# Value products of sixteen attention heads: padded 128-column weights per head against four 32-column strips per group of four heads

## The chip, the cores and the metric

The kernel runs on one NeuronCore of one Trainium2 chip. The metric is the device time of one execution in microseconds (us), from the start of the program to its end on that core; the number given for a kernel is the median of its runs.

## What is computed

Eight sequences of 512 tokens by 512 features pass through four layers. The part that matters here is the attention of the second layer; around it lie a small adapter with a layer norm (before), a feed-forward layer, a second feed-forward layer and a finite-difference stencil (after). Cut to the attention:

```python
x = _ln(src) * (1.0 + scale) + shift
q = (x @ Wq + bq).reshape(B, S, N_HEAD, HEAD_DIM).transpose(0, 2, 1, 3)      # B 8, S 512, 16 heads of 32
k = ...; v = (x @ Wv + bv).reshape(B, S, N_HEAD, HEAD_DIM).transpose(0, 2, 1, 3)
scores = jnp.einsum('bhqd,bhkd->bhqk', q / math.sqrt(HEAD_DIM), k)
scores = scores + attention_bias
scores = jnp.where(src_mask, -jnp.inf, scores.astype(jnp.float32))
probs = jax.nn.softmax(scores, axis=-1).astype(v.dtype)
ctx = jnp.einsum('bhqk,bhkd->bhqd', probs, v)
ctx = ctx.transpose(0, 2, 1, 3).reshape(B, S, D)
x = x + (ctx @ Wo + bo)
```

## The kernel before

The program has two passes. `attention_pass` loops over the eight sequences (adapter, attention, output projection) and writes its rows to memory; `ffn_pass` then does the rest. The change lies in `attention_pass` alone.

Every fp32 operand of a large product is split into two fp16 halves, "hi" and "lo", and a product is three matmuls: hi by hi, hi by lo, lo by hi (the helper `three`).

One iteration of the loop, on TensorE (`pe`): projections q, k, v; transposes of the next sequence's input and its "down" product; then a loop over slots `n` of `SLOTS_ALL` = 75; then the transposes `x1T` of the next sequence and the output projection (`wo`). A slot stands for one head `h` = n // 4 and one block `j` = n % 4 of 128 query rows (there are 64 such blocks). The engines run the same slots in their own program order, tied by semaphores:

- TensorE, slot n: the scores S(n) (two matmuls into one of three PSUM banks 0 to 2: the mask, then q by k), in some slots a product of the next sequence's adapter (`PE_L0`: "up" at 8, 10, 12, 14), the transposes T(n-5) of four probability tiles into a bank of the ring 3 to 5 that the adapter products use too, and the value products PV.
- VectorE (`dve`), slot n: adds the bias to S(n) and takes the row maximum (`negs`, `nmax`), adapter work of some slots (`DVE_L0`: "y" at 9, 11, 13, 15; layer-norm statistics at 19, 21, 23, 25 and 45, 47, 49, 51), then `pT_lo` of T(n-5).
- ScalarE (`act`), slot n: copies T(n-5) from PSUM into `pT_hi`, then the exponential `prob` of S(n), then adapter work (`ACT_L0`: scales at 31, 33, 35, 37 and 56, 58, 60, 62).

The value products give ctx with the features of four heads (a group g) on the 128 partitions of one PSUM bank (6 or 7). A head has only 32 features, so the weights `v_pad` hold, for each head, 128 columns of which 32 are the head's values and 96 are zeros that GpSimd sets once; all matmuls of the group add into the whole bank. They are spread evenly: slot n does key block j of head h for (h, j) = n - 7, three matmuls, and waits for `pT_split` of that block. `pT` holds two heads. When the group's last product is in (`pv_done`), VectorE scales ctx (line 944, slot `ctx_slot(g)` = 16(g+1)+9), ScalarE makes its hi half (line 755, end of that slot) and VectorE its lo half (line 950, start of the next slot). ScalarE waits once per head for `pv_done` before it overwrites `pT_hi`.

`claim` is TensorE's wait for the reader of a bank's last content, `arrived` a reader's wait for the bank to be full.

Of the kernel before, what the change touches and what calls it, by code (L numbers as in the profile page):

```python
# [48 lines left out]
PS = 4096.0  # L49
# [39 lines left out]
LAG_PV = 7  # L89
SLOTS_ALL = HT + 11  # L90


def rinv_slot(g):
    return 4 * T * (g + 1) + 2

# [5 lines left out]
def ctx_slot(g):  # L101
    return 4 * T * (g + 1) + LAG_PV + 2

# [10 lines left out]
def attention_slots():  # L114
# [3 lines left out]
    for n in range(SLOTS_ALL):  # L118
# [9 lines left out]
        if 0 <= n - LAG_PV < HT and (n - LAG_PV) % (4 * T) == 0:  # L128
            g = (n - LAG_PV) // (4 * T)
            order.append((("ctx", g), 6 + g % 2))  # L130
        for g in range(G):
            if n == turn_slot(g):
                order.append((("R", g), 3 + ring % 3))
                ring += 1
# [3 lines left out]
def attention_pass(nc, a, ada_rows, x2_dram):  # L138
# [11 lines left out]
    with ExitStack() as ctx:  # L150
# [38 lines left out]
        v_pad = [sb(f"v_{h}", [P, T, H, P], F16) for h in ("hi", "lo")]  # L189
# [13 lines left out]
        pT = [sb(f"pT_{h}", [P, 2, T, S], F16) for h in ("hi", "lo")]  # L203
# [35 lines left out]
        v_zeroed = sem("v_zeroed")  # L239
# [7 lines left out]
        hi_done = sem("hi_done")  # L247
# [33 lines left out]
        prob_ready = sem("prob_ready")  # L281
        pT_split = sem("pT_split")
# [24 lines left out]
        def read_by(key):  # L307

            name, k = key[0], key[-1]
            return {"xT": (xT_split, C, k), "down": (hid_ready, 2, 0), "expert": (hid_ready, 2, 1),  # L310
                    "up": (y_ready, T, k), "x1T": (x1T_split, C, k), "q": (f32_ready, 12, 0),
                    "k": (f32_ready, 12, 4), "v": (f32_ready, 12, 8), "S": (scored, H * T, k),
                    "T": (pT_split, H * T, k), "R": (rinv_T_ready, G, k), "ctx": (ctx_ready, G, k),
                    "wo": (x2_ready, T, k)}[name]

        def claim(pe, it, key):
# [3 lines left out]
            if last[0] in ("q", "k", "v"):  # L320
                k += last[1]
# [14 lines left out]

        def f32_split(n):

            return (qk_split, 2 * C, n + 1) if n < 8 else (v_split, T, n - 7)

# [111 lines left out]
        def _(pool):  # L452
# [6 lines left out]
            for part in v_pad:  # L459
                pool.memset(part[:, :, :, :].rearrange("p t h m -> p (t h m)").bitcast(F32), 0.0).then_inc(v_zeroed, 1)  # L460
# [61 lines left out]
        def _(pe):  # L522
# [52 lines left out]
            pe.wait_ge(v_zeroed, 2)  # L575
            with pe.Fori(0, B) as it:
# [24 lines left out]
                for n in range(SLOTS_ALL):  # L601
# [29 lines left out]
                    for g in range(G):  # L631
                        if n == turn_slot(g):
# [18 lines left out]
        def _(act):  # L651
# [53 lines left out]
            with act.Fori(0, B) as it:  # L705
                def copy_hi(key, dst, scale):
                    bank = arrived(act, it, key)
                    act.activation(dst, bank[:, :], ACT.Copy, scale=scale).then_inc(hi_done, 1)  # L708

                def to_f32(n, key, func, scale, bias_ap):  # L710
                    bank = arrived(act, it, key)
                    split, per, k = f32_split(n - 2 if n >= 2 else 10 + n)
# [1035 lines left out]
```

## Time and profile before

| what | value |
|---|---|
| median of 3 runs | 3039.82 us (3038.07 to 3041.19) |
| the profiled execution: span from first to last instruction | 3036.2 us |
| TensorE matmul busy | 2699.6 us (89%) |
| VectorE busy | 2182.4 us (72%) |
| ScalarE busy | 1320.3 us (43%) |
| GpSimd busy | 919.8 us (30%) |
| mean granted TensorE clock | 0.966 |

The span is 3.6 us below the median of the runs. The profile gives no device time of its own for the profiled execution beside the span; the 3.6 us are taken as what lies around the span. The attention pass fills the first 1,400 us or so. Matmuls are pipelined: a busy time of TensorE counts each matmul with its latency, so the distance from one start to the next tells what a matmul costs in a stream.

### The profile page before, as it was taken

What the parts mean: (1) busy time and instruction counts of PE and PEld (TensorE: products, weight loads), DVE (VectorE), ACT (ScalarE), POOL (GpSimd) and SP (SyncE); (2) the same over time, 40 slices, a digit from 0 to 9 for tenths busy, and PEclk for the clock granted to TensorE, in tenths of its full rate; (3) what the DMA queues carried; (4) which work ended last, traced back from release to release, by engine and by line L of the source; (5) the groups of instructions that cost most, each with busy time, mean ns of one, the idle gap of its engine ahead of it and who ended that gap; (6) DMA issues with size and microseconds to landing.
All of it is one profiled execution on the core that took longest, in us unless ns stands there. A gap on an engine that the chain in (4) does not pass through costs nothing.

```text
span 3036.2 us, 45734 instructions
## 1 busy us (share of the span) xinstructions
PE 2699.6 (89%) x13435; PEld 1352.2 (45%) x13435; DVE 2182.4 (72%) x4261; ACT 1320.3 (43%) x2485; POOL 919.8 (30%) x898
## 2 busy tenths in 40 slices
PE   2799999999999999994889899998999999999991
PEld 1354555555554545452434344443444434444340
DVE  5686868687877868686866767667676675676758
ACT  2584748576675848584322232222322222222220
POOL 3322131212131312213332513325143350433516
PEclk6899999999999999997999999999999999999995
DMA  3444444353535354443421322222222222222212
GB/s 122 145 153 129 153 133 146 126 153 117 159 131 151 140 144 146 131 153 120 156 91 63 121 86 78 95 75 103 86 91 83 85 96 83 91 89 81 92 59 83
DMA packets 182891, 344.54 MB, mean 113 GB/s; under 512 B 20354, under 2 KB 50690, under 8 KB 182674
## 3 DMA queue, kind: packets, MB, share of 16 engines
q1 hardware_dynamic: 172882, 324.31, 32.9%
q10 hardware_dynamic: 9792, 17.83, 1.6%
q8 instruction: 77, 1.26, 0.2%
q14 instruction: 140, 1.15, 0.1%
HBM read 298.85 MB, written 17.86 MB: 104 GB/s over the span
## 4 chain that ended last, share of the span: by engine, by line
PE 24%; issue 13%; DVE 9%; POOL 7%; ACT 1%; DVEq 0%; DMA 0%; POOLq 0%; SPq 0%; ACTq 0%
PE ffn_bank L1335 7%; PE ffn_bank L1337 7%; PE ffn_bank L1336 7%; POOL prod L1256 3%; DVE g2T_hi L1627 2%; DVE wl_lo L1633 1%; POOL f L1246 1%; POOL x L1274 1%; DVE tmp L1537 1%; POOL prod L1267 1%; PE ffn_bank L1328 1%; DVE g2T_lo L1628 1%; PE ffn_bank L1394 1%; PE ffn_bank L1344 0%; DVE tmp L1577 0%
## 5 line engine op out<-in xcount | busy, mean ns | idle before, releaser
L742 ACT ACTIVATE prob<-negs,nmax 128x512 f32<-128x512 f32 x512 | 368.4, 720 | 113.1 <-DVE nmax L962 112.1
L901 DVE SCALAR_TENSOR_TENSOR pT_lo<-bank,pT_hi 128x512 f16<-128x512 f32 x512 | 350.4, 684 | 93.2 <-ACT pT_hi L708 92.1
L962 DVE CUSTOM_DVE_ANT_0 negs<-bank,bias 128x512 f32<-128x512 f32 x512 | 347.6, 682 | 16.4 <-PE bank L606 12.3
L1627 DVE CAST g2T_hi<-g 128x512 f16<-128x512 f32 x256 | 173.1, 676 | 253.2 <-ACT g L1456 249.9
L616 PE MATMUL bank<-ident,prob 128*128 128x128 f32 x2048 | 312.3, 274 | 37.3 <-ACT prob L742 20.9
L616 PEld LDWEIGHTS bank<-ident,prob 128*128 128x128 f32 x2048 | 250.9, 141 | 160.0 <-ACT prob L742 44.4
L708 ACT ACTIVATE pT_hi<-bank 128x512 f16<-128x512 f32 x512 | 298.3, 583 | 54.3 <-PE bank L616 53.3
L1456 ACT ACTIVATE g<-ffn_bank,bi 128x512 f32<-128x512 f32 x128 | 88.0, 687 | 384.4 <-PE ffn_bank L1337 379.4
L1628 DVE TENSOR_TENSOR g2T_lo<-g,g2T_hi 128x512 f16<-128x512 f32 x256 | 239.7, 936 | 8.8
L1335 PE MATMUL ffn_bank<-w_hi,g2T_hi 128*128 128x512 f16 x512 | 197.1, 385 | 48.2 <-DVE g2T_lo L1628 48.0
L1335 PE MATMUL ffn_bank<-x3T_hi,w_hi 128*128 128x512 f16 x512 | 198.5, 388 | 26.5 <-DVE tmp L1577 25.0
L528 PE MATMUL bank<-pT_hi,v_hi 128*128 128x512 f16 x512 | 195.0, 381 | 18.6 <-DVE pT_lo L901 16.7
L1256 POOL TENSOR_TENSOR prod<-grid,f 128x512 f32<-128x512 f32 x108 | 166.5, 1567 | 125.5 <-DMA grid<-in_grids 119.4
L1337 PE MATMUL ffn_bank<-x3T_hi,w_lo 128*128 128x512 f16 x512 | 199.0, 389 | 0.0
L1336 PE MATMUL ffn_bank<-x3T_lo,w_hi 128*128 128x512 f16 x512 | 198.3, 387 | 0.0
L605 PE MATMUL bank<-mask_add,ident_bf 128*128 128x512 bf16 x512 | 194.6, 380 | 2.4 <-DVE nmax L962 2.4
L1336 PE MATMUL ffn_bank<-w_lo,g2T_hi 128*128 128x512 f16 x512 | 196.1, 383 | 0.0
L1337 PE MATMUL ffn_bank<-w_hi,g2T_lo 128*128 128x512 f16 x512 | 195.7, 382 | 0.0
L606 PE MATMUL bank<-k_st,q_st 96*128 96x512 f16 x512 | 195.6, 382 | 0.0
L1335 PE MATMUL ffn_bank<-x3T_hi,wl_hi 128*128 128x512 f16 x512 | 194.2, 379 | 0.5 <-DVE tmp L1577 0.2
L529 PE MATMUL bank<-pT_lo,v_hi 128*128 128x512 f16 x512 | 194.5, 380 | 0.0
L530 PE MATMUL bank<-pT_hi,v_lo 128*128 128x512 f16 x512 | 194.5, 380 | 0.0
(265 smaller groups left out, 5675.5 us busy)
## 6 DMA issues: line engine op xcount, KB each, us to landing
bias<-in_bias SPq DMA_DIRECT2D x256, 512.0 KB, 3.3
raw<-in_W_l SPq DMA_DIRECT2D x128, 512.0 KB, 3.2
grid<-in_grids SPq DMA_DIRECT2D x172, 256.0 KB, 3.0
xin<-in_x SPq DMA_DIRECT2D x9, 1024.0 KB, 5.2
x2n<-x_rows SPq DMA_DIRECT2D x9, 1024.0 KB, 7.0
out<-outt ACTq DMA_DIRECT2D x36, 256.0 KB, 2.0
q_st<-pT_hi SPq DMA_DIRECT2D x64, 128.0 KB, 4.8
k_st<-pT_hi SPq DMA_DIRECT2D x64, 128.0 KB, 2.8
```

The source lines that it names most:

```text
L606: pe.matmul(bank[:, :], q_st[0:96, h, j * P:(j + 1) * P], k_st[0:96, h, :], start=False, stop=True).then_inc(full_of(("S", h, j)), 1)
L616: mm = pe.transpose(bank[:, t * P:(t + 1) * P], prob[:, h % 2, t, j * P:(j + 1) * P], ident[:, :])
L708: act.activation(dst, bank[:, :], ACT.Copy, scale=scale).then_inc(hi_done, 1)
L742: act.activation(prob[:, h % 2, j, :], negs[:, j % NT, :], ACT.Exp, scale=-1.0, bias=nmax[:, h % 2, j:j + 1], accum_out=rsum[:, j, h:h + 1 ...
L901: ins = dve.scalar_tensor_tensor(out=lo, in0=bank[:, :], scalar=scale, in1=hi, op0=ALU.mult, op1=ALU.subtract)
L962: dve.tensor_tensor_reduce(negs[:, j % NT, :], bank[:, :], bias[:, half % NB, j % 2, :], -1.0, 3.0e38, ALU.add, ALU.min, nmax[:, h % 2, j: ...
L1256: pool.tensor_tensor(prod[:, i, :], grid[:, i, :], f[:, t, :], ALU.mult).then_inc(alpha_prod, 1)
L1335: pe.matmul(out, w[0], x[0], start=first, stop=False)
L1336: pe.matmul(out, w[0], x[1], start=False, stop=False)
L1337: return pe.matmul(out, w[1], x[0], start=False, stop=last)
L1627: link(dve.tensor_copy(gT[0][:, n % 4, :], g32[:, n % 2, :]))
L1628: dve.tensor_tensor(gT[1][:, n % 4, :], g32[:, n % 2, :], gT[0][:, n % 4, :], ALU.subtract)\
```

## The change

The value products of one group are taken together at the group's end. For key block kb of group g (slot `pv_slot(g, kb)` = 16g + 20 + kb) TensorE now issues twelve matmuls: for each of the three hi/lo pairs, one matmul for each of the four heads, with weights of 32 columns (`v_sp`, unpadded) and an output of 32 partitions (`bank[32 i : 32 i + 32]`). Every matmul still streams 512 columns over 128 rows, and there are still 192 of them in an iteration. `pT` holds five heads. `pv_done` counts groups instead of heads, and ScalarE waits for it ahead of every copy. `ctx_slot(g)` becomes 16g + 24, one slot earlier than before. GpSimd's two zero fills are gone, and VectorE writes v's halves to contiguous tiles.

```diff
-LAG_PV = 7
+LAG_PV = 3
+RING_H = 5
+def pv_slot(g, kb):
+    return T * (4 * g + 3) + kb + LAG_T + LAG_PV
+def groups_before(h):
+    return (h - RING_H) // 4 + 1 if h >= RING_H else 0
 def ctx_slot(g):
-    return 4 * T * (g + 1) + LAG_PV + 2
+    return pv_slot(g, T - 1) + 1
...
-        v_pad = [sb(f"v_{h}", [P, T, H, P], F16) for h in ("hi", "lo")]
+        v_sp = [sb(f"v_{h}", [P, T, D], F16) for h in ("hi", "lo")]
...
-        pT = [sb(f"pT_{h}", [P, 2, T, S], F16) for h in ("hi", "lo")]
+        pT = [sb(f"pT_{h}", [P, RING_H, T, S], F16) for h in ("hi", "lo")]
...
-            for part in v_pad:
-                pool.memset(part[:, :, :, :].rearrange("p t h m -> p (t h m)").bitcast(F32), 0.0).then_inc(v_zeroed, 1)
...
-                    if 0 <= n - LAG_PV < HT:
-                        h, j = (n - LAG_PV) // T, (n - LAG_PV) % T
-                        key = ("ctx", h // 4)
-                        if h % 4 == 0 and j == 0:
-                            claim(pe, it, key)
-                            pe.wait_ge(v_split, 1 + it * T + T)
-                        bank = psum[banks.place[key][0]]
-                        pe.wait_ge(pT_split, 1 + it * HT + T * h + j + 1)
-                        mm = three(bank[:, :], [v[:, j, h, :] for v in v_pad], [p[:, h % 2, j, :] for p in pT],
-                                   h % 4 == 0 and j == 0, h % 4 == 3 and j == T - 1)
-                        if j == T - 1:
-                            mm.then_inc(pv_done, 1)
                     for g in range(G):
+                        for kb in range(T):
+                            if n != pv_slot(g, kb):
+                                continue
+                            key = ("ctx", g)
+                            if kb == 0:
+                                claim(pe, it, key)
+                                pe.wait_ge(v_split, 1 + it * T + T)
+                            bank = psum[banks.place[key][0]]
+                            pe.wait_ge(pT_split, 1 + it * HT + T * (4 * g + 3) + kb + 1)
+                            for w, x in ((0, 0), (0, 1), (1, 0)):
+                                for i in range(4):
+                                    h = 4 * g + i
+                                    mm = pe.matmul(bank[HD * i:HD * i + HD, :], v_sp[w][:, kb, h * HD:(h + 1) * HD],
+                                                   pT[x][:, h % RING_H, kb, :], start=kb == 0 and w + x == 0,
+                                                   stop=kb == T - 1 and w == 1)
+                            if kb == T - 1:
+                                mm.then_inc(pv_done, 1)
...
-                        if j == 0:
-                            act.wait_ge(pv_done, 1 + it * H + max(0, h - 1))
-                        copy_hi(("T", h, j), pT[0][:, h % 2, j, :], PS)
+                        bank = arrived(act, it, ("T", h, j))
+                        act.wait_ge(pv_done, 1 + it * G + groups_before(h))
+                        act.activation(pT[0][:, h % RING_H, j, :], bank[:, :], ACT.Copy, scale=PS)\
+                            .then_inc(pT_hi_ready, 1)
```

TensorE's order around slots 19 to 21 (the transposes `ident,rinv_x` stand in slot 20). Before, each slot has its three value products:

```order
L605 MATMUL bank<-mask_add,ident_bf 128x512
L606 MATMUL bank<-k_st,q_st 128x512
L616 MATMUL bank<-ident,prob 128x128 x4
L528 MATMUL bank<-pT_hi,v_hi 128x512
L529 MATMUL bank<-pT_lo,v_hi 128x512
L530 MATMUL bank<-pT_hi,v_lo 128x512
L637 MATMUL bank<-ident,rinv_x 128x128 x4
```

The same place after the change, from the scores of slot 19:

```order
L603 MATMUL bank<-mask_add,ident_bf 128x512
L604 MATMUL bank<-k_st,q_st 128x512
L614 MATMUL bank<-ident,prob 128x128 x4
L331 REGISTER_ALU
L603 MATMUL bank<-mask_add,ident_bf 128x512
L604 MATMUL bank<-k_st,q_st 128x512
L614 MATMUL bank<-ident,prob 128x128 x4
L630 MATMUL bank<-pT_hi,v_hi 32x512 x4
L630 MATMUL bank<-pT_lo,v_hi 32x512 x4
L630 MATMUL bank<-pT_hi,v_lo 32x512 x4
L640 MATMUL bank<-ident,rinv_x 128x128 x4
```

Slot 19 now has scores and transposes alone; slot 20 has twelve value products in place of three.

VectorE's order where ctx of group 0 is taken (`L962`, after the change `L945`, is the bias addition of a slot; `L901`, after it `L954`, is pT_lo). Before, slots 25 and 26:

```order
L944 SCALAR_TENSOR_TENSOR ctx<-bank,rinv_T 128x512
L331 REGISTER_ALU
L960 REGISTER_ALU
L962 ISA negs,nmax<-bank,bias 128x512
L962 ISA nmax 128x1
L849 BN_STATS stats<-xin 128x6
L772 REGISTER_ALU
L851 BN_AGGR mv<-stats 128x2
L901 SCALAR_TENSOR_TENSOR pT_lo<-bank,pT_hi 128x512
L949 REGISTER_ALU
L950 SCALAR_TENSOR_TENSOR xT_lo<-ctx,bv,xT_hi 128x512
```

After, slots 24 and 25:

```order
L927 SCALAR_TENSOR_TENSOR ctx<-bank,rinv_T 128x512
L337 REGISTER_ALU
L941 ISA
L943 REGISTER_ALU
L945 ISA negs,nmax<-bank,bias 128x512
L945 ISA nmax 128x1
L954 SCALAR_TENSOR_TENSOR pT_lo<-bank,pT_hi 128x512
L933 SCALAR_TENSOR_TENSOR xT_lo<-ctx,bv,xT_hi 128x512
```

The statistics that stood between ctx and its lo half in slot 25 now stand behind the lo half.

## Rows read from the trace of the kernel before

**Rows 1.** The page, part 5: the engines' idle time before three groups of the slots.

```profile
L901 DVE SCALAR_TENSOR_TENSOR pT_lo<-bank,pT_hi 128x512 f16<-128x512 f32 x512 | 350.4, 684 | 93.2 <-ACT pT_hi L708 92.1
L962 DVE CUSTOM_DVE_ANT_0 negs<-bank,bias 128x512 f32<-128x512 f32 x512 | 347.6, 682 | 16.4 <-PE bank L606 12.3
L708 ACT ACTIVATE pT_hi<-bank 128x512 f16<-128x512 f32 x512 | 298.3, 583 | 54.3 <-PE bank L616 53.3
```

The columns of a window: stretch, its length, busy us (instructions) of PE, PE's weight loads, VectorE, ScalarE, GpSimd, granted clock, DMA share, GB/s.

**Rows 2.** Window of the 75 slots of the fifth iteration.

```profile
622.53:738.00 115.47, 106.38 (x608) 63.07 (x607) 98.14 (x230) 93.42 (x210) 27.07 (x48) 1.00 0.44 146
```

**Rows 3.** Timeline of slots 9 to 12 (start us, us, engine, line).

```profile
635.66 0.69 DVE L845 SCALAR_TENSOR_TENSOR xin<-bank,xin 128x512 f32<-128x512 f32 x1
...
636.40 0.39 PE L528 MATMUL bank<-wup_hi,ctx 128*128 128x512 f16 x1 [0.24 <-DVE xin L845]
...
637.06 0.60 PE L616 MATMUL bank<-ident,prob 128*128 128x128 f32 x4
637.50 0.38 PE L528 MATMUL bank<-pT_hi,v_hi 128*128 128x512 f16 x1
637.70 0.60 ACT L708 ACTIVATE pT_hi<-bank 128x512 f16<-128x512 f32 x1 [1.11 <-PE bank L616]
...
638.15 0.38 PE L605 MATMUL bank<-mask_add,ident_bf 128*128 128x512 bf16 x1
...
638.33 0.69 DVE L901 SCALAR_TENSOR_TENSOR pT_lo<-bank,pT_hi 128x512 f16<-128x512 f32 x1 [0.78 <-ACT pT_hi L708]
...
638.58 0.60 PE L616 MATMUL bank<-ident,prob 128*128 128x128 f32 x4
639.02 0.38 PE L528 MATMUL bank<-pT_hi,v_hi 128*128 128x512 f16 x1
...
639.64 0.69 DVE L845 SCALAR_TENSOR_TENSOR xin<-bank,xin 128x512 f32<-128x512 f32 x1
```

**Rows 4.** Timeline of ScalarE in slot 16.

```profile
649.04 0.60 ACT L708 ACTIVATE pT_hi<-bank 128x512 f16<-128x512 f32 x1 [0.50 <-PE bank L616]
```

**Rows 5.** Timeline of VectorE, slots 19 to 26.

```profile
655.26 0.66 DVE L901 SCALAR_TENSOR_TENSOR pT_lo<-bank,pT_hi 128x512 f16<-128x512 f32 x1
...
658.58 0.66 DVE L901 SCALAR_TENSOR_TENSOR pT_lo<-bank,pT_hi 128x512 f16<-128x512 f32 x1
...
663.69 0.68 DVE L944 SCALAR_TENSOR_TENSOR ctx<-bank,rinv_T 128x512 f32<-128x512 f32 x1
...
665.83 0.66 DVE L901 SCALAR_TENSOR_TENSOR pT_lo<-bank,pT_hi 128x512 f16<-128x512 f32 x1
666.58 0.75 DVE L950 SCALAR_TENSOR_TENSOR xT_lo<-ctx,bv,xT_hi 128x512 f16<-128x512 f32 x1
```

**Rows 6.** Line 950 over the whole program: idle of VectorE before it (us, times).

```profile
  ACT xT_hi L755: 21.4, 24
```

**Rows 7.** Timeline of TensorE around the 8-row matmul of the second pass.

```profile
1522.29 0.38 PE L1328 MATMUL ffn_bank<-msp_lo,dmat 128*128 128x512 f16 x1
1522.60 0.39 PE L1328 MATMUL ffn_bank<-halo,halo_w 8*128 8x512 f16 x1
1522.92 0.39 PE L1335 MATMUL ffn_bank<-x3T_hi,w_hi 128*128 128x512 f16 x1
```

**Rows 8.** Timeline of the end of the slots, VectorE then TensorE.

```profile
736.48 0.69 DVE L901 SCALAR_TENSOR_TENSOR pT_lo<-bank,pT_hi 128x512 f16<-128x512 f32 x1 [0.39 <-ACT pT_hi L708]
...
738.03 1.91 PE L534 MATMUL bank<-ident,xin 128*128 128x128 f32 x16
```

**Rows 9.** Windows, a sparse stretch and its successor, then another sparse stretch.

```profile
229.50:232.90 3.40, 1.56 (x9) 0.47 (x7) 2.54 (x7) 2.79 (x7) 1.20 (x1) 1.00 0.00 0
233.00:236.40 3.40, 3.40 (x12) 2.04 (x13) 2.35 (x7) 3.00 (x7) 2.55 (x2) 0.51 0.02 5
393.40:396.80 3.40, 1.98 (x11) 0.81 (x9) 2.54 (x7) 2.32 (x5) 0.73 (x1) 1.00 0.00 0
```

**Rows 10.** Timeline of GpSimd, its first operation after the zero fills.

```profile
24.48 5.82 POOL L490 TENSOR_TENSOR xin<-xin,up_b 128x512 f32<-128x512 f32 x4 [15.75 <-DMA bo<-in_bo]
```

More of the change, by code:

```diff
@@ L48 @@
 NEG = -1.0e30
-PS = 4096.0
 RSQRT_SEED = 1597463007.0
@@ L127, in attention_slots @@
             ring += 1
-        if 0 <= n - LAG_PV < HT and (n - LAG_PV) % (4 * T) == 0:
-            g = (n - LAG_PV) // (4 * T)
-            order.append((("ctx", g), 6 + g % 2))
         for g in range(G):
+            if n == pv_slot(g, 0):
+                order.append((("ctx", g), 6 + g % 2))
             if n == turn_slot(g):
@@ L281, in attention_pass @@
         prob_ready = sem("prob_ready")
+        pT_hi_ready = sem("pT_hi_ready")
         pT_split = sem("pT_split")
@@ L307, in read_by @@
         def read_by(key):
-            name, k = key[0], key[-1]
+            name, k = key[0], key[-1] if len(key) > 1 else 0
             return {"xT": (xT_split, C, k), "down": (hid_ready, 2, 0), "expert": (hid_ready, 2, 1),
[L311 to L314, printed above, removed]
+                    "up": (y_ready, T, k), "x1T": (x1T_split, C, k), "q": (f32_ready, 12, k),
+                    "k": (f32_ready, 12, 4 + k), "v": (f32_ready, 12, 8 + k), "S": (scored, H * T, k),
+                    "T": (pT_split, H * T, k), "R": (rinv_T_ready, G, k),
+                    "ctx": (ctx_ready, G, k), "wo": (x2_ready, T, k)}[name]
         def claim(pe, it, key):
@@ L808, in weight_lo @@
                                          op0=ALU.mult, op1=ALU.subtract).then_inc(weights_split, 1)
-            def diagonal(v, t):
-                part = v[:, t, :, :]
-                return bass.AP(tensor=part.tensor, offset=part.offset,
-                               ap=[list(part.ap[0]), [4 * P, G], [P + HD, 4], [1, HD]])
             def l0_part(link, it, part):
@@ L893, in _ @@
                 link = chained(it * LINKS_A + before)
-                def lo_of(key, k, hi, lo, signal, scale=None):
-                    bank = psum[banks.place[key][0]]
-                    dve.wait_ge(hi_done, it * (H * T) + k + 1)
-                    if scale is None:
-                        ins = dve.tensor_tensor(lo, bank[:, :], hi, ALU.subtract)
-                    else:
-                        ins = dve.scalar_tensor_tensor(out=lo, in0=bank[:, :], scalar=scale, in1=hi,
-                                                       op0=ALU.mult, op1=ALU.subtract)
-                    ins.then_inc(signal, 1)
                 def split_f32(k, hi, lo, signal):
@@ L924, in _ @@
                     dve.wait_ge(f32_ready, it * 12 + 2 * C + t + 1)
-                    src = f32t[:, t % 2, :].rearrange("p (g i d) -> p g i d", i=4, d=HD)
-                    hi, lo = (diagonal(v, t) for v in v_pad)
-                    link(dve.tensor_copy(hi, src))
-                    dve.tensor_tensor(lo, src, hi, ALU.subtract).then_inc(v_split, 1)
+                    link(dve.tensor_copy(v_sp[0][:, t, :], f32t[:, t % 2, :]))
+                    dve.tensor_tensor(v_sp[1][:, t, :], f32t[:, t % 2, :], v_sp[0][:, t, :], ALU.subtract)\
+                        .then_inc(v_split, 1)
                 dve.wait_ge(v_split, 1 + it * T + T)
@@ L940, in _ @@
                             bank = psum[banks.place["ctx", g][0]]
-                            dve.wait_ge(pv_done, 1 + it * H + 4 * g + 4)
+                            dve.wait_ge(pv_done, 1 + it * G + g + 1)
                             dve.wait_ge(rinv_T_ready, it * G + g + 1)
@@ L968, in _ @@
                         h, j = (n - LAG_T) // T, (n - LAG_T) % T
-                        lo_of(("T", h, j), n - LAG_T, pT[0][:, h % 2, j, :], pT[1][:, h % 2, j, :], pT_split, PS)
+                        bank = psum[banks.place["T", h, j][0]]
+                        dve.wait_ge(pT_hi_ready, it * HT + n - LAG_T + 1)
+                        dve.scalar_tensor_tensor(out=pT[1][:, h % RING_H, j, :], in0=bank[:, :], scalar=PS,
+                                                 in1=pT[0][:, h % RING_H, j, :], op0=ALU.mult, op1=ALU.subtract)\
+                            .then_inc(pT_split, 1)
                 for c in range(C):
```

30 lines of the change are left out of this document (11 added, 19 removed).

## Prediction

> **What bounds the kernel now.** I read the page first. TensorE is busy 89% of the span, and a window over the slots of one iteration shows it 106.4 us busy in 115.5 [rows 2]. That invites the naive sum: one value product batch of a slot takes 637.50 to 638.15 = 0.65 us, 64 of them 41.6 us, and a quarter of it would be left if four strips ran side by side. The second view is the idle time by releaser, which says whether anybody waits for TensorE. VectorE waits before pT_lo for ScalarE's pT_hi, 93.2 us in all, and before the bias addition hardly at all: 12.3 us for TensorE, 1.5 us an iteration. ScalarE waits 53.3 us for transposes, 6.7 us an iteration [rows 1]. So TensorE can return at most 6.7 + 1.5 us an iteration to the others, whatever it saves itself. The third view is the timeline, to see which of these waits has the value products behind it.
>
> Slots 9 to 15 (adapter "y" in every second slot) are a ring of dependences. y starts at 635.66; "up" of the next tile needs y's bank and starts at 636.40, right at y's end; the transposes follow at 637.06, pT_hi at 637.70, pT_lo at 638.33, and with the next bias addition behind it the next y at 639.64 [rows 3]. The links are 0.74 + 0.66 + 0.64 + 0.63 + 1.31 = 3.98 us for two slots, exactly the distance of the two y. The value products stand behind the transposes and are no link. ScalarE's wait of 1.11 us for transposes there (three such cycles) is a wait for "up", not for them.
>
> From slot 17 to slot 63 ScalarE does not wait for TensorE at all in the iteration that I read. With statistics in every second slot, VectorE needs 655.26 to 658.58 = 3.32 us for two slots, 1.66 a slot [rows 5], where TensorE's slot costs 0.65 + 0.43 (scores, 638.15 to 638.58) + 0.44 (transposes, 638.58 to 639.02) = 1.52 us [rows 3]. TensorE is nearly full, but VectorE and ScalarE, handing rows to each other, set the pace.
>
> **The change, part by part.** *Twelve strips in place of twelve full matmuls.* TensorE's sum of matmuls is the same, 192 an iteration. A batch costs 12 x 0.217 = 2.6 us if strips run one after the other and 0.65 us if four run at once; no row shows two strips at once. To that comes the change of the array's shape: the one matmul with 8 weight rows starts 0.31 us after its predecessor and its successor 0.32 us after it, instead of 0.217 [rows 7], so I add 0.10 us at each end. I take 0.65 + 0.20 = 0.85 us a batch, 13.6 us an iteration. TensorE then has 28 us less to do, 224 us in all, and I expect almost none of it in the time. The Trainium skill, "TensorE: Matmul & The Clock Gate", Part 3, reports 2.38x for three column tiles of 32 by 512; scaled to four that is about 3.2x, 0.82 us by an estimate from that page, and with the ends 1.0 us. No run here shows it so far; my sum would not change by it.
>
> *Removal from slots 7 to 19 and so on.* In the y cycles 0, by the links above. Leaving them, ScalarE waits 0.50 us for transposes that stand behind value products [rows 4]; VectorE gets back between 0 and 0.50, I take 0.35 us, since part of its own queue lies behind. Later slots: 0, hidden under VectorE.
>
> *Bunching in slots 20 to 23 of a group.* A slot costs TensorE 0.87 + 0.85 = 1.72 us there, against 1.66 of VectorE, four times: 0.24 us late, with TensorE one to two slots ahead (three score banks): 0.
>
> *ctx one slot earlier.* This is the part with a price. For group 0 ctx is taken at 663.69, and statistics of the same slot cover ScalarE's turn, so that the lo half starts at 666.58, 0.09 us behind the end of pT_lo (665.83 + 0.66) [rows 5]. In slot 24 there are no statistics. The other groups have no cover and wait 21.4 us in 24 times, 0.89 us each [rows 6], which says what the uncovered turn costs. Group 0 joins them: +0.85 us on VectorE, the engine that sets the pace; bounds 0 (if the covered slot gives the same time back) and 1.3. Group 1 lies between slots without extra work either way: 0. In group 2 ScalarE's scale now stands ahead of its turn and the wait grows, but the same 0.8 us of scale delayed the pT_hi behind it before: 0. Queued behind the waiting lo half are the bias addition and pT_lo of that slot.
>
> *The end of the slots.* Transposes are no longer spaced by value products, but four batches now stand behind the last of them. The last pT_lo ends at 737.17 and the next phase begins at 738.03 [rows 8]. Four batches, the transposes of the sums (0.44) and the changes of shape (0.2 to 0.3) are 3.3 us after a last transpose that I put, from my walk through the timeline, at about 734.5: 737.9, 0.05 to 0.1 us earlier. Bound on the good side 0.7.
>
> *The rest at nothing.* The zero fills of GpSimd lie before 24.48 - 15.75 = 8.7 us, where it begins to wait 15.75 us for a transfer [rows 10]; uncovered they would be at most these 8.7 us, once. ScalarE's wait for pv_done ahead of every copy rides on the copy and adds no instruction; the ring of five asks for the products of slot 23 in slot 25. The writes of v's halves lie under full projections.
>
> Sum for an iteration: -0.35 + 0.85 - 0.05 = +0.45 us; times eight +3.6 us. The profiled execution goes from 3036.2 to 3039.8, and with the 3.6 us around the span the time is **3043.4 us**. The bounds of the terms (-0.5 - 0.7 to +1.3, times eight) give 3030 to 3050; a few falls of the clock (below) stretch it to 3056.
>
> **Rivals.** *B, strips overlap only in part.* The nearest row for short pairs of load and matmul is the transposes: four in 0.44 us, 0.11 each [rows 3]. Twelve are 1.3, a batch 1.5 us. Slots 20 to 23 then cost TensorE 2.4 us each against 1.66; less its lead, +0.5 us in group 0 and about +2 in group 2, whose slots have less other work; the end grows by 4 x 0.65 = 2.4 us. Together +5.3 an iteration: 3083 us. The end decides first: a batch over 0.75 us costs there.
>
> *C, no overlap.* A batch is 2.8 us, a slot 3.67: four slots 14.7 against 6.6 less a lead of 3, +5 us in each of three groups, +7.6 at the end, 23 us an iteration: 3225 us; with every load exposed (0.31 each, rows 7) about 3350. For it speaks that no row shows overlap. The same page of the Trainium skill says in Part 3 that a weight load overlaps matmuls in flight only in another row group; the four strips share theirs. In this trace loads do overlap within one row group (matmuls at 0.217 us with a load each), so I weigh it low.
>
> *D, TensorE is the bound after all.* If all 6.7 us of ScalarE's waits came back [rows 1], eight times that less the ctx term is 47 us: 2993 us. For it: 92% busy in the slots. Against: the links of the y cycle close without value products.
>
> *E, the clock.* A stretch with 1.56 us busy in 3.4 was followed by a granted clock of 0.51; one with 1.98 kept 1.00 [rows 9]. A slot without value products leaves about 1.2 us busy in 1.66, so 2.4 in 3.4 us, but around ctx's wait about 1.8, between the two. A fall to 1.2 GHz makes a slot 1.74 us, a lead hides that; in y cycles it adds 0.66 + 0.44 and batches cost as in B. With the clock low half of the time, some 4 us an iteration: 3075 us, always low 3105. The page says too (Part 4) that transposes do not hold the clock up; by that the low share would be the larger one; the rows do not decide.
>
> **How the numbers follow.** Chances: my case 0.64, B 0.11, C 0.10, D 0.08, E 0.07. Within 0.2% (6 us, about what a measurement of this kernel can tell) lie 3034 to 3046: 0.44 of my case; 0.04 of it lies below and 0.16 above. Faster 0.04 + D = 0.12; same 0.44; slower 0.16 + B + C + E = 0.44. The range 3026 to 3100 takes my case, B and E, and leaves out C and D. My case's own range is 3030 to 3056.
>
> **What would show it.** A batch's twelve starts within 0.65 to 0.85 us; starts 0.217 apart mean C. TensorE busy down, its idle time before transposes and scores up, by 20 us and more an iteration. The y still 3.98 us apart. Idle before the ctx lo half in 32 cases instead of 24, some 28 us. ScalarE's wait for transposes still near 50 us. If that wait falls to a few us and the time with it, D is right. A clock below 0.95 in the slots means E.

## The result, and the profile after

| | before | after |
|---|---|---|
| median | 3038.32 us (3036.86 to 3041.19, 9 runs) | 3046.91 us (3044.43 to 3050.80, 9 runs) |
| ratio | | 1.0029, 95% interval 1.0019 to 1.0038 |
| profiled span | 3036.2 us | 3046.6 us |
| mean granted TensorE clock | 0.966 | 0.939 |

The change makes the kernel 0.29% slower. 3046.91 lies in the predicted case's own range (3030 to 3056), 3.5 us above its 3043.4, on the slower side of the 0.2% bound. (What the text above calls the fifth iteration is the fourth of eight. The 3.6 us that it takes as lying around the span are 1.8 us in the profiled execution of the change, 3048.37 less 3046.6.)

The page of the kernel after, part 5; L954 is pT_lo, L945 the bias addition, L738 pT_hi, L614 the transposes, L603 the mask matmul of the scores [rows 1 for before]:

```profile
L614 PE MATMUL bank<-ident,prob 128*128 128x128 f32 x2048 | 355.1, 303 | 114.1 <-DVE pT_lo L954 56.1
L954 DVE SCALAR_TENSOR_TENSOR pT_lo<-bank,pT_hi 128x512 f16<-128x512 f32 x512 | 349.3, 684 | 90.9 <-ACT pT_hi L738 90.8
L945 DVE CUSTOM_DVE_ANT_0 negs<-bank,bias 128x512 f32<-128x512 f32 x512 | 347.5, 682 | 17.3 <-PE bank L604 12.3
L738 ACT ACTIVATE pT_hi<-bank 128x512 f16<-128x512 f32 x512 | 298.4, 584 | 47.3 <-PE bank L614 46.2
L603 PE MATMUL bank<-mask_add,ident_bf 128*128 128x512 bf16 x512 | 212.9, 416 | 48.2 <-DVE nmax L945 48.1
```

The three waits of VectorE and ScalarE are nearly those of before (93.2, 16.4, 54.3 us; ScalarE's is 7 us shorter). TensorE's own idle time is what grew: 114.1 + 48.2 us here, where the page of before has 37.3 + 2.4 for the same groups. The relief went into waiting.

Windows of the kernel after: the fourth iteration from its first scores to the x1T transposes (against [rows 2], which begins 0.22 us earlier, at the mask matmul), a stretch inside it, one at its end, and the whole third iteration:

```profile
624.07:741.49 117.42, 90.44 (x608) 51.80 (x606) 97.67 (x230) 93.79 (x210) 27.14 (x48) 0.90 0.43 144
...
672.07:676.07 4.00, 4.00 (x17) 2.87 (x16) 3.57 (x10) 3.33 (x9) 1.38 (x7) 0.50 0.71 237
736.00:738.00 2.00, 2.00 (x11) 1.63 (x9) 1.72 (x4) 1.41 (x3) 0.02 (x1) 0.50 1.01 343
...
458.98:575.31 116.33, 88.45 (x607) 49.97 (x605) 97.47 (x230) 93.66 (x210) 27.15 (x48) 0.93 0.43 145
```

In the fourth iteration TensorE is busy 16 us less than before, the stretch is 2.14 us longer when both are counted from the same matmul, and the granted clock is 0.90 instead of 1.00: it falls to half (1.2 GHz) three to five times in each iteration. The iterations are not alike. Leaving the first aside: the second, fourth, fifth and seventh have a fall at their end and are 2.1 to 2.4 us longer than before; the third, sixth and eighth have none there and are only about 1.1 us longer.

Timeline of TensorE around the first batch of a group:

```profile
660.36 0.60 PE L614 MATMUL bank<-ident,prob 128*128 128x128 f32 x4
660.89 0.40 PE L630 MATMUL bank<-pT_hi,v_hi 128*32 128x512 f16 x4
661.11 0.39 PE L630 MATMUL bank<-pT_lo,v_hi 128*32 128x512 f16 x4
661.33 0.39 PE L630 MATMUL bank<-pT_hi,v_lo 128*32 128x512 f16 x4
661.65 0.39 PE L603 MATMUL bank<-mask_add,ident_bf 128*128 128x512 bf16 x1
```

Four strips start together ("x4"; their starts lie within 0.01 us), and each hi/lo pair starts 0.22 us behind the last. The transposes ahead of the batch take 0.53 instead of 0.44 us, and 661.33 to 661.65 is 0.32 instead of 0.22. The batch is 0.66 + 0.09 + 0.10 = 0.85 us, as predicted.

Line 933 (ctx's lo half) over the whole program, and the end of the slots on the timeline:

```profile
  ACT xT_hi L757: 33.6, 32
```

```profile
734.57 3.57 PE L614 MATMUL bank<-ident,prob 128*128 128x128 f32 x16 [2.23 <-DVE pT_lo L954]
...
741.49 1.20 PE L533 MATMUL bank<-ident,xin 128*128 128x128 f32 x9
```

Timeline of VectorE in two of the slots with "y" (against [rows 3]):

```profile
637.06 0.69 DVE L841 SCALAR_TENSOR_TENSOR xin<-bank,xin 128x512 f32<-128x512 f32 x1
...
639.73 0.69 DVE L954 SCALAR_TENSOR_TENSOR pT_lo<-bank,pT_hi 128x512 f16<-128x512 f32 x1 [0.78 <-ACT pT_hi L738]
640.33 0.68 DVE L945 CUSTOM_DVE_ANT_0 negs<-bank,bias 128x512 f32<-128x512 f32 x1
...
640.94 0.69 DVE L841 SCALAR_TENSOR_TENSOR xin<-bank,xin 128x512 f32<-128x512 f32 x1
```

The two y lie 3.88 us apart, 0.10 us less than before: the link from pT_lo to the next y is 1.21 instead of 1.31 us. Why it is shorter stays open.

All 32 turns of ctx now wait, 12.2 us more than the 24 of [rows 6]. At the end TensorE waits 2.23 us, and its last 16 transposes then run at half clock.

**Where the 10.4 us of the spans are.** The first scores start at 126.18 instead of 130.47 us: 4.3 us won ahead of the loop. From there to the last x1T transposes (1404.42 instead of 1393.93) 14.8 us are lost, 1.85 us an iteration; what follows is equal. The loss, from the starts of VectorE's bias additions in the fourth iterations of both traces (column 1: us after the first scores before the change; column 2: how much later after it):

```text
 37.6  -0.54   behind the y cycles (-0.40 in them, -0.22 on leaving)
 48.4  +0.28   behind ctx of group 0                    (+0.82)
 54.4  +0.89   behind a stretch at half clock           (+0.61)
 89.0  +0.79   group 1 passed
106.9  +1.34   behind group 2                           (+0.55)
115.3  +2.14   x1T transposes; last transposes at half clock  (+0.80)
```

### The profile page after: what moved, and what is told of

Its sections match the earlier page's. It is cut to its first block, busy times and chain, and to the rows that moved or that the text cites. A ratio compares the mean times of both kernels' runs of the same rounds, so it can differ in the third digit from the quotient of the medians.

```text
span 3046.6 us, 46067 instructions
## 1 busy us (share of the span) xinstructions
PE 2568.7 (84%) x13435; PEld 1259.3 (41%) x13435; DVE 2179.7 (72%) x4261; ACT 1323.9 (43%) x2485; POOL 916.7 (30%) x896
## 4 chain that ended last, share of the span: by engine, by line
PE 24%; issue 13%; DVE 9%; POOL 7%; ACT 1%; DVEq 0%; DMA 0%; POOLq 0%; SPq 0%; ACTq 0%
PE ffn_bank L1322 7%; PE ffn_bank L1324 7%; PE ffn_bank L1323 7%; POOL prod L1243 3%; DVE g2T_hi L1614 2%; DVE wl_lo L1620 1%; POOL f L1233 1%; POOL x L1261 1%; DVE tmp L1524 1%; POOL prod L1254 1%; PE ffn_bank L1315 1%; PE ffn_bank L1381 1%; DVE g2T_lo L1615 1%; PE ffn_bank L1331 0%; DVE tmp L1564 0%
## 5 line engine op out<-in xcount | busy, mean ns | idle before, releaser
L614 PE MATMUL bank<-ident,prob 128*128 128x128 f32 x2048 | 355.1, 303 | 114.1 <-DVE pT_lo L954 56.1
L954 DVE SCALAR_TENSOR_TENSOR pT_lo<-bank,pT_hi 128x512 f16<-128x512 f32 x512 | 349.3, 684 | 90.9 <-ACT pT_hi L738 90.8
L614 PEld LDWEIGHTS bank<-ident,prob 128*128 128x128 f32 x2048 | 273.3, 156 | 279.6 <-ACT prob L744 117.1
L945 DVE CUSTOM_DVE_ANT_0 negs<-bank,bias 128x512 f32<-128x512 f32 x512 | 347.5, 682 | 17.3 <-PE bank L604 12.3
L738 ACT ACTIVATE pT_hi<-bank 128x512 f16<-128x512 f32 x512 | 298.4, 584 | 47.3 <-PE bank L614 46.2
L603 PE MATMUL bank<-mask_add,ident_bf 128*128 128x512 bf16 x512 | 212.9, 416 | 48.2 <-DVE nmax L945 48.1
L604 PE MATMUL bank<-k_st,q_st 96*128 96x512 f16 x512 | 211.8, 414 | 0.0
L1322 PE MATMUL ffn_bank<-wl_hi,g2T_hi 128*128 128x512 f16 x512 | 194.0, 379 | 0.0
L1323 PE MATMUL ffn_bank<-wl_lo,g2T_hi 128*128 128x512 f16 x512 | 194.0, 379 | 0.0
L1324 PE MATMUL ffn_bank<-wl_hi,g2T_lo 128*128 128x512 f16 x512 | 194.0, 379 | 0.0
```

The source lines that it names most:

```text
L603: pe.matmul(bank[:, :], ident_bf[:, :], mask_add[:, j, :], start=True, stop=False)
L614: mm = pe.transpose(bank[:, t * P:(t + 1) * P], prob[:, h % 2, t, j * P:(j + 1) * P], ident[:, :])
L738: act.activation(pT[0][:, h % RING_H, j, :], bank[:, :], ACT.Copy, scale=PS)\
L945: dve.tensor_tensor_reduce(negs[:, j % NT, :], bank[:, :], bias[:, half % NB, j % 2, :], -1.0, 3.0e38, ALU.add, ALU.min, nmax[:, h % 2, j: ...
L954: dve.scalar_tensor_tensor(out=pT[1][:, h % RING_H, j, :], in0=bank[:, :], scalar=PS, in1=pT[0][:, h % RING_H, j, :], op0=ALU.mult, op1=AL ...
L1322: pe.matmul(out, w[0], x[0], start=first, stop=False)
```

## The experiments

Each kernel was timed against the kernel before on the same chip. "Period" is the mean distance from the first scores of an iteration to the next iteration's q projection, worked out from the timeline (seven iterations): 128.38 us before, 130.34 after the change. A period belongs to one profiled execution, a median to all of them, and the two need not agree: the 1.96 us between these periods would be 15.7 us in eight iterations.

**ctx one slot later.**

```diff
 def ctx_slot(g):
-    return pv_slot(g, T - 1) + 1
+    return pv_slot(g, T - 1) + 2
```

> The changed kernel with ctx taken at slot 16g + 25 again, as before the change; everything else stays changed. Theory 1 (the earlier ctx is the largest term of the loss in the slots: pT_lo falls behind by 0.8 us between slots 23 and 26 of the iteration read, and by 0.5 around slots 56 to 59): 0.8 to 1.3 us less in each of eight iterations, 6 to 10 us faster than the changed kernel, 3037 to 3041 us. VectorE's wait before the lo half goes from 32 times back to 24. Theory 2 (the loss is TensorE's: batches of twelve and a low clock; the wait before the lo half only stands where another wait stood): within 2 us of the changed kernel, 3045 to 3049.

3036.68 us (ratio 0.9992, 0.9983 to 1.0001), 10 us below the change; period 128.39, in an execution of 3033.11 us, the fastest of its eleven. Line 933 there, and VectorE with ctx's lo half behind statistics again:

```profile
  ACT xT_hi L757: 18.8, 24
```

```profile
659.25 0.69 DVE L845 BATCH_NORM_STATS2 stats<-xin 128x6 f32<-128x512 f32 x1
...
660.19 0.66 DVE L954 SCALAR_TENSOR_TENSOR pT_lo<-bank,pT_hi 128x512 f16<-128x512 f32 x1
660.83 0.75 DVE L933 SCALAR_TENSOR_TENSOR xT_lo<-ctx,bv,xT_hi 128x512 f16<-128x512 f32 x1
```

With ctx back in its slot the whole loss in the loop is gone. Batches and strips cost nothing in sum: the 0.5 us won in and behind the y cycles are lost again further on.

**Which group.** The same for group 0 alone: `+ (2 if g == 0 else 1)`.

> The change with ctx of group 0 alone one slot later (slot 25, as before), the other three groups as in the change. The prediction put the whole price on group 0, 0.85 us an iteration, and nothing on groups 1 to 3: if that is so, the time lies 6.8 us below the change's and about where e1 is, 3037 to 3041, with 24 waits of the lo half and not 32. The timeline of the change showed another 0.55 us at group 2: then e11 keeps these, 4.4 us above e1: 3040 to 3043. Rival 'the clock': the falls of the slots 24 to 31 come from ctx of group 0 being early, each costing 1.27 us where the extra work was in (e5); then e11 gains both, and x1T lies 1.2 to 2 us earlier.

3036.09 us (0.9996, 0.9987 to 1.0005); the medians don't tell it from the kernel with all four. Period 129.04: by the periods 1.30 of the 1.95 us are group 0's, and the wait of the lo half is 26.3 us in 24 times. This split is rough, since the profiled execution here (3039.61 us) is the second slowest of its eleven, and that of the kernel with all four the fastest. The iterations without a fall at their end agree better: from first scores to x1T 115.34 us here and 115.14 with all four late, so groups 1 to 3 are worth 0.2 us there. Group 0 is most of it, as predicted.

**The zero fills.** Into the changed kernel, two fills of the same length (into `pT`) were put back; in the kernel before they were moved behind VectorE's first operations.

```diff
# the change, with two fills
+            for part in pT:
+                pool.memset(part[:, 0:4, :, :].rearrange("p h t s -> p (h t s)").bitcast(F32), 0.0).then_inc(zeroed, 1)
...                                          # waits for zeroed ahead of the loop
# before, fills late
+            pool.wait_ge(dom_clipped, 1)
             for part in v_pad:
```

> The changed kernel with GpSimd's two zero fills of 128 x 4096 fp32 words put back at their old place, into the probability tiles, which are written later anyway. Theory 1 (the first conversion on VectorE waits behind the fills, and the loads behind it start late): the prologue is 5 to 6 us longer, 3052 to 3053 us. Theory 2 (the 5.3 us by which the changed kernel reaches its first projections earlier come from transfers that happened to land sooner): the time stays within 2 us of 3047.

> The kernel before the change, with one line more: GpSimd waits for dom_clipped ahead of its zero fills, so that VectorE's first chain and the loads that wait for it do not meet the fills. Theory 1: 5 to 6 us faster than the kernel before, 3032.5 to 3033.5 us, with the same padded weights and the same order of value products. Theory 2 (transfers by chance): within 2 us of 3038.3. If the fills now stop another operation of VectorE for long, the gain is smaller than 5.

3051.40 us (1.0040, 1.0026 to 1.0054) and 3033.94 us (0.9985, 0.9976 to 0.9994); first scores at 130.74 and 125.29 us. GpSimd and VectorE's first operation, before:

```profile
1.77 3.51 POOL L460 MEMSET v_hi<- 128x4096 f32 x1
5.22 3.51 POOL L460 MEMSET v_lo<- 128x4096 f32 x1
```

```profile
3.62 5.14 DVE L778 CAST steps<-steps_i 128x8 f32<-128x8 int32 x1 [3.62 <-DMA freq<-in_freqs]
```

and with the fills late:

```profile
7.56 3.51 POOL L461 MEMSET v_hi<- 128x4096 f32 x1 [5.73 <-DVE dom_at L803]
```

```profile
3.61 0.17 DVE L779 CAST steps<-steps_i 128x8 f32<-128x8 int32 x1 [3.61 <-DMA freq<-in_freqs]
```

A conversion of 8 columns lasts 5.14 us while GpSimd fills, until the fills end at 8.7 us, and 0.17 us otherwise; the loads that hang on `dom_at` come as much later. The Trainium skill, "SBUF — State Buffer", section "Who interferes with whom", says that VectorE's casts can take a port pair shared with GpSimd, that whoever issues first has it for its whole instruction, and that the other blocks. The trace agrees that the cast, which comes second, is held (from 3.62 us), and it shows that it is held until both fills are over, not only the one that was running.

**The order of the twelve matmuls.** Strips outside, pairs inside:

```diff
-                            for w, x in ((0, 0), (0, 1), (1, 0)):
-                                for i in range(4):
+                            for i in range(4):
+                                for w, x in ((0, 0), (0, 1), (1, 0)):
```

> The changed kernel with the two loops of a batch exchanged: the three products of one head's strip follow each other, then those of the next, so that consecutive matmuls use the same strip. Same matmuls, same waits. Theory 1 (four matmuls run at once only because they alternate between strips): starts of one strip lie 0.217 us apart, a batch takes 2.6 us or, where the next strip's first may start at once, somewhere between 0.65 and 2.6; at 2.6 the working of case C gives 20 us an iteration, some 3200 us. Theory 2 (TensorE reaches ahead over the three of a strip): a batch stays near 0.65 us and the time within 5 us of 3047.

3048.28 us (1.0029, 1.0018 to 1.0039), period 130.33, as the change. The program now gives three matmuls of one strip before the next strip, and still four strips start together:

```profile
661.13 0.42 PE L630 MATMUL bank<-pT_hi,v_hi 128*32 128x512 f16 x4
661.35 0.41 PE L630 MATMUL bank<-pT_lo,v_hi 128*32 128x512 f16 x4
661.57 0.41 PE L630 MATMUL bank<-pT_hi,v_lo 128*32 128x512 f16 x4
661.91 0.39 PE L603 MATMUL bank<-mask_add,ident_bf 128*128 128x512 bf16 x1
```

**One strip per slot.** The kernel before with unpadded weights of 32 columns (its zero fills are a quarter as long, and the first scores start at 125.20 us):

```diff
-                        mm = three(bank[:, :], [v[:, j, h, :] for v in v_pad], ...
+                        mm = three(bank[HD * i:HD * i + HD, :], [v[:, j, h, :] for v in v_pad], ...
...                                          # i = h % 4; v_pad and its writes have 32 columns a head
```

> The kernel before, with its order, three value products in every slot, but unpadded weights of 32 columns and one strip of 32 partitions each; the zero fills are a quarter as long. No two strips are side by side, and every slot has two changes of the array's shape. My theory of 0.10 us for a change of shape: TensorE's slot grows from 1.52 to 1.7 us, against VectorE's 1.66; the clock stays near 0.966 or rises, and the time lies 0 to 8 us above e3's (3034), since most of the 0.2 us is hidden: 3034 to 3042; shorter fills give about 4 of the 5.3 us of the prologue. Rival 'a strip matmul is slower': starts 0.3 us apart in every slot, TensorE's slot at 1.9 us sets the pace: 3060 and more. Rival 'the shape costs nothing': starts 0.217 apart throughout, 3033 to 3036.

3079.24 us (1.0140, 1.0124 to 1.0155), period 133.94: far outside what I expected. Timeline of a slot and window of the slots:

```profile
642.51 0.39 PE L528 MATMUL bank<-pT_hi,v_hi 128*32 128x512 f16 x1
642.73 0.38 PE L529 MATMUL bank<-pT_lo,v_hi 128*32 128x512 f16 x1
642.95 0.38 PE L530 MATMUL bank<-pT_hi,v_lo 128*32 128x512 f16 x1
643.26 0.39 PE L605 MATMUL bank<-mask_add,ident_bf 128*128 128x512 bf16 x1
```

```profile
633.93:754.76 120.83, 117.28 (x608) 55.25 (x606) 99.99 (x230) 95.61 (x210) 27.03 (x48) 1.00 0.43 140
```

Inside the strip the starts stay 0.22 us apart, so a matmul of 32 columns is no slower. The unit price was right (0.1 us at each end, 0.2 a slot), its effect was not: 64 x 0.2 = 12.8 us an iteration, of which TensorE's 9 us of slack [rows 2] absorb only 7.2, and it is busy 117.3 of 120.8 us. Making TensorE's slot cheaper gains nothing, but making it 0.2 us dearer makes it the bound.

**Keeping TensorE busy.** One extra mask matmul in each slot without value products (52 an iteration) and eight ahead of the transposes of the last four slots, all overwritten; then the same with ctx late; then ctx late with the eight alone (`FILL` is 1, 1 and 0, `FILL_END` 8).

```diff
+                        if n < 16 or n % 16 not in (4, 5, 6, 7):
+                            for _ in range(FILL):
+                                pe.matmul(bank[:, :], ident_bf[:, :], mask_add[:, j, :], start=True, stop=True)
...
+                    if n == HT + 1:
+                        pe.wait_ge(scored, 1 + it * HT + HT - 2)
+                        for _ in range(FILL_END):
+                            pe.matmul(psum[(HT - 3) % 3][:, :], ident_bf[:, :], mask_add[:, 0, :], start=True, stop=True)
```

> The kernel after the change, with more work for TensorE and the same result: in every slot without value products one extra mask matmul (0.22 us) into the scores bank, overwritten by the next, and eight extra matmuls (1.7 us) ahead of the last four transposes, where TensorE waits 2.23 us now. Theory 'clock': of the excess of about 1.9 us an iteration some 0.6 us in slots 31 to 39 and 0.8 to 1.4 us at the end come from the stretches at half clock (3 to 4 an iteration). Then the granted clock rises from 0.939 to over 0.96, the distance from the first scores to the x1T transposes falls from about 117.1 us to 115.5 to 116.3 us, and the time lies 6 to 12 us below the change's: 3034 to 3041. Rival 'the clock falls are harmless': the clock rises, but the time stays at 3045 to 3048. Rival 'TensorE's slots count': 48 extra matmuls an iteration are 10.4 us of TensorE; if a part of them shows in the time, it is 3050 and more.

> The same extra work, and ctx one slot later (slot 16g + 25). If the price of ctx (about 10 us in all with its neighbours) and that of the clock are independent, this is e1's 3036.7 less 6 to 12 us: 3025 to 3031, below both kernels. If e1's gain and the filler's are largely the same microseconds (ctx one slot later already removed stretches at half clock, which rose from 0.939 to 0.948 there), it is 3033 to 3037.

> e1 (the change with ctx one slot later) and only the eight extra matmuls ahead of the last four transposes, none in the other slots. If the half clock at the end of the slots is what the end costs (four transposes and four batches took 6.9 us from 734.57 to 741.49, where the links give 3.3 to 4), this gives 0.8 to 1.4 us an iteration: 3026 to 3031, about as e6. If the falls in the middle of the slots matter as much, it lies 3 to 5 us above e6. If the last transposes are late for VectorE's and ScalarE's sake, the end does not move: 3036 to 3038, as e1.

3045.56 us (1.0025, 1.0016 to 1.0034), 3037.56 us (0.9998, 0.9988 to 1.0007) and 3034.21 us (0.9987, 0.9978 to 0.9996). The first kernel has iterations with and without a fall. Windows of its third and fourth, four microseconds at the same place in both, then the whole of both:

```profile
505.16:509.16 4.00, 4.00 (x26) 2.52 (x24) 3.82 (x11) 3.71 (x9) 1.36 (x7) 1.00 0.73 233
670.01:674.01 4.00, 4.00 (x15) 2.38 (x14) 3.24 (x9) 3.17 (x8) 1.38 (x7) 0.50 0.76 239
457.16:573.04 115.88, 93.30 (x666) 51.95 (x664) 97.48 (x230) 93.10 (x210) 27.15 (x48) 1.00 0.44 146
622.01:739.16 117.15, 95.98 (x666) 53.58 (x665) 97.77 (x230) 93.22 (x210) 27.16 (x48) 0.97 0.43 144
```

The starts of their bias additions agree within 0.01 us up to the fall; behind it those of the fourth iteration come 1.25 to 1.29 us later, to the end. That is what one fall behind group 0's batches costs in this kernel, with ctx early and extra matmuls. With ctx late and the same extra matmuls, windows of the second and the fourth iteration are

```profile
289.01:405.62 116.61, 97.77 (x666) 56.34 (x665) 98.20 (x230) 93.42 (x210) 27.33 (x48) 0.94 0.45 145
618.76:733.92 115.16, 94.39 (x666) 53.36 (x665) 97.85 (x230) 93.10 (x210) 27.34 (x48) 0.99 0.45 146
```

The second has three falls and loses 1.45 us by them; the fourth has a single one, 103 us in. So a late ctx does not make every fall cheap. Where a fall begins decides: with ctx late and no extra matmuls, a fall behind group 0's batches costs 0, 0.23 and 0.35 us when it begins 47.6, 47.0 and 46.6 us into the iteration, and such an iteration takes 115.14 us in all. That falls cost time where TensorE is already being waited for fits this, but is not shown. Free of falls up to there, ctx late is worth 115.88 - 115.16 = 0.72 us an iteration.

In the total, keeping the clock up bought nothing that can be told. With ctx early the median is 1.4 us below the change's and the intervals overlap (the extra matmul ahead of every first score takes 0.2 us an iteration of its own); with ctx late all the extra matmuls give nothing. The eight alone gave 2.5 us, at the edge of what can be told, and not at the end: from the last bias addition to x1T it is 8.34 us with them and without.

**The last group in halves.** Heads 12 and 13 in slots 60 to 63, heads 14 and 15 in slots 68 to 71, on top of ctx late; then with the eight extra matmuls too.

```diff
+                    kb = n - pv_slot(G - 1, 0) + 2 * T
+                    if 0 <= kb < T:
+                        ...                      # strips 0 and 1 of group 3, three products each
...
-                                for i in range(4):
+                                for i in (range(4) if g < G - 1 else range(2, 4)):
```

> e1 (ctx one slot later), and in the last group alone the value products in two halves: heads 12 and 13 (two strips, six matmuls a block) in slots 60 to 63, heads 14 and 15 in slots 68 to 71. In e1 the x1T transposes start 4.00 us after the last transposes of probabilities (728.81 to 732.81), of which the three batches of the end are 2.06 and the first 0.76; before it was 2.82. Theory 'the end is TensorE's': two strips side by side halve each batch (0.33 us), the distance falls by 1.2 to 1.3 us until the last pT_lo (ends 731.2) sets it, x1T comes 1.0 to 1.2 us earlier, 8 to 9.5 us in all: 3027 to 3029. Rival 'two strips do not run two at once' (six matmuls 0.217 apart, 1.3 us a batch): the end grows by 2.2 us an iteration, 3054. Rival 'the end is VectorE's': no change, 3035 to 3038.

> e9 with the eight extra matmuls ahead of the last four transposes (as in e8). The extra matmuls keep the clock up at the end: e8's x1T came 115.1 us after the first scores on average, e1's 115.5. If both effects are independent: 3024 to 3027, below every kernel so far. If the last pT_lo sets the end in both, it equals e9.

3037.94 us (1.0001, 0.9992 to 1.0010) and 3047.65 us (1.0034, 1.0023 to 1.0045). The expectation had an error: a batch lasts as long as one strip's three matmuls, with two strips as with four, so halving the strips could not shorten it. (The next one compares 115.1 with 115.5 us; counted alike they are 115.1 and 115.3.) Timeline of the first:

```profile
730.83 1.86 PE L614 MATMUL bank<-ident,prob 128*128 128x128 f32 x12 [0.26 <-ACT prob L757]
...
733.49 0.39 PE L643 MATMUL bank<-pT_hi,v_hi 128*32 128x512 f16 x2
733.71 0.38 PE L643 MATMUL bank<-pT_lo,v_hi 128*32 128x512 f16 x2
733.93 0.38 PE L643 MATMUL bank<-pT_hi,v_lo 128*32 128x512 f16 x2
...
736.88 1.31 PE L533 MATMUL bank<-ident,xin 128*128 128x128 f32 x10
```

From the first of the last 16 transposes to x1T it is 6.05 us here, 6.07 with four strips and ctx late (726.74 to 732.81), and 6.13 before (731.90 to 738.03). At full clock the end costs what it cost before. The second kernel is 10 us slower because its extra matmuls stand in the way there. Timeline of TensorE and ScalarE at its end:

```profile
733.43 1.89 PE L614 MATMUL bank<-mask_add,ident_bf 128*128 128x512 bf16 x8
735.16 1.04 PE L623 MATMUL bank<-ident,prob 128*128 128x128 f32 x8
```

```profile
735.79 1.57 ACT L760 ACTIVATE pT_hi<-bank 128x512 f16<-128x512 f32 x3 [1.56 <-PE bank L623]
```

With ctx late alone, TensorE waits 1.3 us or more ahead of the last 16 transposes, and with the eight matmuls too it still waits 0.5 to 0.7 us there. With the last group in halves it waits only 0.1 to 0.3 us there; the eight matmuls delay the transposes, ScalarE waits 1.5 us for them, and from the last bias addition to x1T each of the eight iterations takes 9.05 instead of 7.65 to 7.81 us, 10 to 11 us in all.

**"up" behind the transposes.** ctx late, and `l0_products(it, PE_L0[n])` moved from ahead of the slot's transposes to behind them.

> e1 (the change with ctx one slot later), and in slots 8, 10, 12 and 14 TensorE issues the product 'up' behind the transposes of the slot and not ahead of them. It tests the prediction's reading of slots 9 to 15: a ring y, up, transposes, pT_hi, pT_lo, bias addition, y of 3.98 us for two slots, in which 'up' and its wait for y's bank are the link and the value products are none. If that is right, the transposes no longer wait for y, the two slots fall towards VectorE's 3.32 us of other slots (plus nothing for y, which stands in place of statistics), and four such pairs give 2 to 2.6 us an iteration: 3016 to 3021 us, 16 to 21 below e1's 3036.7, with ScalarE's wait for transposes falling from about 45 us to 20 or less. Rival 'the next ring is as long' (y waits for up, which now stands 0.44 us later, and VectorE's queue waits behind y): 3034 to 3044. Rival 'ScalarE or the bias transfers set these slots': 3034 to 3038.

3017.81 us (3017.69 to 3019.62; ratio 0.9934, 0.9921 to 0.9948), the fastest version: 20 us below the kernel before, 29 below the change. Its page and timeline (y, ScalarE's pT_hi):

```profile
L738 ACT ACTIVATE pT_hi<-bank 128x512 f16<-128x512 f32 x512 | 296.7, 581 | 20.7 <-PE bank L612 19.5
```

```profile
625.01 0.69 DVE L841 SCALAR_TENSOR_TENSOR xin<-bank,xin 128x512 f32<-128x512 f32 x1
...
628.02 0.69 DVE L841 SCALAR_TENSOR_TENSOR xin<-bank,xin 128x512 f32<-128x512 f32 x1
```

The y come 3.01 us apart instead of 3.88 with ctx late alone (3.98 before, [rows 3]), and the period falls from 128.39 to 126.30. The ring through "up" was what held slots 9 to 15.

## Why the prediction came out as it did

The likeliest case held in mechanism and sign. Its number, 3043.4 against 3046.9, is in part luck: it is a sum with errors in both directions, and it stands on a base of 3039.8 us where the median of nine runs before is 3038.3. As a difference, 3.6 us were forecast and 8.6 measured.

- **Strips four at once, 0.85 us a batch:** right. B and C are out, by rows of the change and of the strip-by-strip order.
- **TensorE's relief worth almost nothing:** right. ScalarE's wait for transposes is 46.2 us (53.3 before), and TensorE's idle time before transposes and scores rose by 122.6 us, 15 an iteration where I had put 20 or more. Rival D asked for the wait to fall to a few us; it did fall to 19.5 us when "up" was moved, in a kernel whose value products are unchanged.
- **In the y cycles 0, leaving them -0.35 us:** measured -0.40 and -0.22 (with +0.08 ahead of them -0.54). The y did not stay 3.98 us apart; they come every 3.88 us. The ring itself is as I read it: moving "up" behind the transposes opened it.
- **ctx of group 0, +0.85 us:** right: +0.82 in the table. Between the two iterations without an earlier fall it is 0.91 behind group 0, of which 0.72 are left at the end for all four groups. The trace and an edit both show it.
- **Groups 1 to 3 at nothing:** group 1 was right. Group 2 was mis-sized: 0.55 us. With ctx late the same stretch still loses 0.34 us, so ctx's slot is only a part of it; the rest stays open.
- **The end, -0.05 us:** right at full clock (-0.06 with ctx late, and -0.05 in the change's own iterations without a fall there). In four of its eight iterations it was +0.80 to +1.09, with the clock at half. (The working put the start of x1T at 737.9; its own terms give 734.5 + 3.3 = 737.8, 0.2 us early.)
- **The zero fills at nothing:** the step that failed. I named as their cover GpSimd's own wait for a transfer, and never asked whom they hold up. They held up VectorE by 5 us and with it the loads that wait for `dom_at`: 4.3 us to the first scores (5.2 with the fills late, 4.6 with them back in the change).
- **The clock (case E, 0.07):** its sign came, falls in every iteration and a clock of 0.90 in the slots, but not its time of 3075. Some of the half clock costs nothing: with ctx late, the bias additions ahead of the fall some 74 us in and behind it stand equally far (-0.41 us) from those of the kernel before. My case stretched its range for a few falls and put them at 0 in the sum. In the fourth iteration 0.61 + 0.80 of its 2.14 us stand at stretches of half clock; in the third, with no fall at its end, 0.38 of 1.06 us. That the mean loss an iteration is 1.85 and not 0.45 us is this, group 2, and nothing else that I can name.
- **Sums of the rivals:** B's 4 x 0.65 is 2.6, not 2.4, and C's end is 4 x 1.95 = 7.8, not 7.6; B would be some 3084 us. No choice between the cases hangs on it.

In sum: predicted +0.45 an iteration and 0 ahead of the loop; measured +1.85 and -4.3. The two misses, +11.2 and -4.3 us, leave the 7 us by which the span is above its forecast of 3039.8. ctx early and the falls are not independent: the 0.72 us of ctx without falls and the 1.95 us with them say that with the late ctx the falls of these kernels cost less. In its trace the fall at the very end is missing from the third iteration on; why the falls come where they do stays open.

## What to carry to other kernels

Making the engine with the highest busy share cheaper gives nothing if the trace shows no one waiting for it; here 28 us less work an iteration gave back at most 0.6 us, while one product moved behind another off a ring of dependences gave 15 us of span. When operations are bunched, look at what else moves by a slot with them (here ctx, out from under the statistics that covered it). When an operation is removed, ask who was held up by it, also on engines that share no semaphore with it. Extra work put into a wait is free only as long as the wait is there: the same eight matmuls cost nothing in one kernel and 10 us in the next.

## What the hardware showed that I had not expected

- Four strips of 32 columns run side by side even when the program gives three matmuls of one strip before those of the next (0.22 us for four starts either way). Two strips take as long as four.
- A change between 32-column and 128-column weights costs 0.1 us each way; once per slot (two changes each) the iteration is 5.6 us longer, once per block of a group no loss can be seen.
- Two fills by GpSimd, one behind the other, stretch a 0.17 us conversion of VectorE to 5.14 us.
- A fall of the clock at about the same place of an iteration costs between 0 and 1.27 us. In one and the same trace it is nothing or 0.35 us, by whether the fall begins 47.6 or 46.6 us into the iteration.
